# Mixer: VectorE runs the angle reduction behind the third chunk's states instead of ahead of them

## The chip, the cores and the metric

The kernel runs on one core of a Trainium2 chip. The metric is the device time of one execution in microseconds; the median of the runs is compared. The core has TensorE (PE, with its weight loads as PEld), VectorE (DVE), ScalarE (ACT), GpSimd (POOL) and SyncE (SP), whose queue issues every DMA here. Each engine works through its own instructions in order; semaphores tie them together.

## The reference

The input is x of shape (16, 512, 128). Six blocks are applied one after another: a feed-forward (FFN) block, attention, the same FFN, a mixture FFN, a state-space mixer, and the mixture FFN again. The part around the change is the mixer:

```python
proj = x @ W_in                                  # z, x_raw, B, C, dt_raw, lam_raw, theta
x_raw = silu(x_raw)
Bm, Cm = rms(B) * B_norm_bias, rms(C) * C_norm_bias
dt = clip(softplus(dt_raw + dt_bias), 0.0001, 0.5)
ang = -cumsum(mean(dt, -1) * theta, axis=1)      # 32 angles per token
cos, sin = cos(ang), sin(ang)
Cr, Br = rope(Cm, cos, sin), rope(Bm, cos, sin)
alpha = exp(dt * A); lam = sigmoid(lam_raw)
# chunked scan: S = decay * S + state of the chunk; y = intra + inter part
y = rms(y * silu(z)) @ W_out
```

and the mixture FFN, whose eight experts are relu(x @ W_e + b_e), summed with weights counted over the whole input.

## The kernel before, in words

Three phases follow each other: `attention_phase` (first FFN, attention, second FFN), `mixer_phase` (first mixture FFN and mixer), `last_ffn_phase`. The change touches only `mixer_phase`.

One batch is 512 tokens, four tiles of 128. The mixer phase runs 19 iterations, and each works on up to four batches at once: the experts of batch i (`ffn`), the preparation of batch i - 1 (`prep`: projection, step sizes, angles, rotation, scores), the scan of batch i - 2 (`scan`: four chunks), and the output of batch i - 3 (`tail`). From the third to the sixteenth iteration at least scan, preparation and experts are there together; in the seventeenth the experts are not.

The order of the work is written out by hand. `MIXER_AT` gives each step one or more slots from 0 to 82, and every engine walks through the slots of an iteration in turn (`for q in range(SLOTS)`) and issues what is due there. Within a slot VectorE takes tail, scan, ffn and prep in that order. The slots that matter here: `sums` 41, `angles` 49, `chunks` 50 (the third), `states` 56 (the third), `weights` 56, `own` 58 (the fourth), `experts` 59 and 64 (the last two), `products` 65 (the third), `rotate` 65, `chunks_rest` 66 (the third), `sumT` 68, `turn_y` 69, `own_p` 70, `diagonal_p` 71, `chunks` 73 (the fourth), `bt` 73.

- `sums` (TensorE, L1559): matmuls into banks 3 and 4 give the decay exponents, the summed angles (bank 4, columns 128 to 256) and the shifted weights.
- `angles` (VectorE, L1111): three clamps of the exponents to `mid`, then L1120 and L1121 read the angles from the bank to `ang` (the second with pi/2 added, for the cosine), then `reduce_angle` (L816): five operations in place on 128 x 256 elements, L819 to L823, each waiting for the one before it. The last signals `ang`.
- `decays` (ScalarE, L1347, slot 49): four Exp, then a table load (L1361), then the Sin (L1363), which waits for `ang`. Behind it in ScalarE's order stand `own_token` (L1366, slot 58) and the Relu of the last expert (L1396, slot 64).
- `states` (VectorE, L1171): for the two halves of a chunk a multiplication with the decay (L1179) and an addition of the chunk's matmuls from PSUM (L1186). `chunk_rest` on TensorE (L1615) waits for them, and `products` (L1191) on VectorE for `chunk_rest`.
- `add_experts` (GpSimd, L1484, slot 64) adds the last Relu to the one before; `sumT` on TensorE (L1704) sums the experts through matmuls with the identity (L1711) and waits for it.
- `rotate`: VectorE (L1135) and GpSimd (L1468) each multiply and add one half; VectorE then copies (L1145) when GpSimd's half is there, and TensorE transposes the result (L1579).
- `diagonal` on GpSimd (L1479) multiplies B and C (L1481).

On VectorE, `wait(ins)` counts the instruction on the semaphore `dve` and waits for it; `mark(ins)` only counts it and returns the count.

Of the kernel before, what the change touches and what calls it, by code (L numbers as in the profile page):

```python
# [18 lines left out]
ALU = mybir.AluOpType  # L19
# [796 lines left out]
def reduce_angle(v, wait, r, k):  # L816


    wait(v.tensor_scalar(k, r, float(1 / (2 * np.pi)), ROUND, ALU.mult, ALU.add))  # L819
    wait(v.tensor_scalar(k, k, ROUND, None, ALU.subtract))  # L820
    wait(v.scalar_tensor_tensor(r, k, -TWO_PI_HI, r, ALU.mult, ALU.add))
    wait(v.scalar_tensor_tensor(r, k, -TWO_PI_LO, r, ALU.mult, ALU.add))
    return v.tensor_scalar(r, r, PI_F32, -PI_F32, ALU.min, ALU.max)  # L823
# [93 lines left out]
def layer1_views(place):  # L917
# [17 lines left out]
    "gated": (34, 44, 73, 80), "squares": (25, 45, 66, 75), "mean": (35, 66, 77, 82), "mean_read": 82,  # L935
    "experts": (15, 17, 22, 25, 36, 44, 59, 64), "sumT": 68, "y": 71, "stats2": 73, "xn2": 74, "turn2": 80,
    "low2": 82, "project": (1, 2, 3, 6), "gates": 11, "shift": 7, "soft": 15, "steps": 34, "norm_bc": 15, "sums": 41,
    "angles": 49, "weights": 56, "rotate": 65, "diagonal": 74, "diagonal_p": 71, "bt": 73, "scores": 75, "mask": 78,
}


def mixer_phase(nc, x_in, n_in, x_out, n_out, w, ew, cnt_acc):
# [4 lines left out]
    with ExitStack() as ctx:  # L947
        def sb(name, shape, dt=F32):
            return ctx.enter_context(nc.sbuf_tensor("m_" + name, shape, dt))
# [25 lines left out]
        ang, angk, sc = (sb(n, [P, 2, NT, M_HEADS]) for n in ("ang", "angk", "sc"))  # L975
# [5 lines left out]
        bt = sb("bt", [P, 2, NT, 2, P])  # L981
# [27 lines left out]
        S = {n: ctx.enter_context(nc.semaphore("m_" + n)) for n in [*PER, "x_in0", "x_in1", "x_out0", "x_out1", "n_in0", "n_in1", "n_out", "dve", "pool", "start", "counted", "weights", "rate"]}  # L1009
# [3 lines left out]
        AT = MIXER_AT  # L1013
# [8 lines left out]
        def all_of(name, b):  # L1022
            return PER[name] * (b + 1)

        def batches(i):

            return [b if 0 <= b < BATCH else None for b in (i, i - 1, i - 2, i - 3)]

        with nc.Block(no_gpsimd_drain=True) as block:
# [25 lines left out]
            def _(dve):  # L1055
                v, done = nc.vector, [0]

                def mark(ins):
                    done[0] += 1
                    ins.then_inc(S["dve"], 1)  # L1060
                    return done[0]

                def wait(ins):
                    dve.wait_ge(S["dve"], mark(ins))
# [46 lines left out]
                def angles(b):  # L1111
                    dve.wait_ge(S["prep_ps"], all_of("prep_ps", b))
                    pa = ps[:, 4, 128:256].rearrange("p (t h) -> p t h", t=NT)
                    v.tensor_scalar(mid[:, 0], ps[:, 3, 384:512].rearrange("p (t h) -> p t h", t=NT),
                                    CLAMP, None, ALU.min)
                    v.tensor_scalar(mid[:, 2], ps[:, 3, 384:512].rearrange("p (t h) -> p t h", t=NT),
                                    -CLAMP, None, ALU.max)
                    v.tensor_scalar(mid[:, 1], ps[:, 4, 0:128].rearrange("p (t h) -> p t h", t=NT),
                                    CLAMP, None, ALU.min).then_inc(S["mid"], 1)
                    v.tensor_copy(ang[:, 0], pa)  # L1120
                    wait(v.tensor_scalar(ang[:, 1], pa, float(np.pi) / 2, None, ALU.add))  # L1121
                    reduce_angle(v, wait, ang[:, :], angk[:, :]).then_inc(S["ang"], 1)

                def source_weights(b):
# [83 lines left out]
                def mean_square(b):  # L1208
                    dve.wait_ge(S["ms_mm"], all_of("ms_mm", b))
                    v.tensor_scalar(ms[:, :], ps[:, 5, 256:264:2], 1.0 / D_INNER, RMS_EPS, ALU.mult,  # L1210
                                    ALU.add).then_inc(S["ms"], 1)

                def output(b):
                    dve.wait_ge(S["wo"], all_of("wo", b))
                    dve.wait_ge(S["rms"], all_of("rms", b))
                    if b >= 2:
                        dve.wait_ge(S[f"x_out{b % 2}"], 16 * (b // 2))
                    for t in range(NT):
                        ins = v.scalar_tensor_tensor(y2[:, b % 2, t, :], ps[:, 5, P * t:P * t + P], rms[:, t:t + 1],
                                                     y[:, b % 4, t, :], ALU.mult, ALU.add)  # L1220
                    ins.then_inc(S["y2"], 1)
# [23 lines left out]
                wait(v.tensor_scalar(w["w_in"][:], w["w_in"][:], W_SCALE, None, ALU.mult))  # L1245
                wait(v.tensor_copy(w["w_in_hl"][:, 0], w["w_in"][:]))
                v.tensor_tensor(w["w_in_hl"][:, 1], w["w_in"][:], w["w_in_hl"][:, 0], ALU.subtract).then_inc(S["weights"], 1)
                coef_done = [0, 0]
                for i in range(ITERATIONS):
                    ffn, prep, scan, tail = batches(i)  # L1250
                    for q in range(SLOTS):
                        if tail is not None:
                            if q == AT["out"]:
                                output(tail)
                            if q == AT["stats_gate"]:
                                dve.wait_ge(S["y2"], all_of("y2", tail))
                                statistics(y2[:, tail % 2], 1, S["var2"])
                            if q == AT["gate"]:
                                dve.wait_ge(S["gate"], all_of("gate", tail))
                                v.tensor_tensor(gl[:, :, :], ps[:, 5, 0:NT * EXPERTS].rearrange(  # L1260
                                    "p (t e) -> p t e", t=NT), w["gate_b"][:, :, :], ALU.add).then_inc(S["gate_read"], 1)
                            if q == AT["top"]:
                                dve.wait_ge(S["gate_read"], all_of("gate_read", tail))
                                top_two(v, dve, S["dve"], mark, gl, g8, gix, gif)
                                count_choices(v, dve, S["dve"], mark, gif, onehot, w, cnt_acc)
                        if scan is not None:
                            if q in AT["variants"]:
                                variants(scan, AT["variants"].index(q))
                            if q in AT["states"]:
                                states(scan, AT["states"].index(q))  # L1270
                            if q in AT["products"]:
                                products(scan, AT["products"].index(q))
                            if q in AT["gated"]:
                                gated(scan, AT["gated"].index(q))
                            if q == AT["mean_read"]:
                                mean_square(scan)
                        if ffn is not None:
                            if q in AT["experts"] and AT["experts"].index(q) % 2 == 0:
                                expert(ffn, AT["experts"].index(q))
                            if q == AT["low2"]:  # L1280
                                dve.wait_ge(S["xh"], all_of("xh", ffn))
                                v.tensor_tensor(xhl[:, 1], ps[:, 2, :], xhl[:, 0], ALU.subtract).then_inc(S["xl"], 1)
                            if q == AT["y"]:
                                dve.wait_ge(S["sumT"], all_of("sumT", ffn))
                                dve.wait_ge(S[f"x_in{ffn % 2}"], 16 * (ffn // 2 + 1))
                                v.scalar_tensor_tensor(y[:, ffn % 4], ps[:, 2, :].rearrange("p (t d) -> p t d", t=NT), 1.0 / EXPERT_SCALE,
                                                       x[:, ffn % 2], ALU.mult, ALU.add).then_inc(S["y"], 1)
                            if q == AT["stats2"]:
                                dve.wait_ge(S["y"], all_of("y", ffn))
                                statistics(y[:, ffn % 4], 0, S["var"])  # L1290
                        if prep is not None:
                            if q == AT["shift"]:
                                shift_dt(prep)
                            if q == AT["steps"]:
                                steps(prep)
                            if q == AT["angles"]:
                                angles(prep)
                            if q == AT["weights"]:
                                source_weights(prep)
                            if q == AT["rotate"]:  # L1300
                                rotate(prep)
                            if q == AT["diagonal"]:
                                diagonal(prep)
                            if q == AT["mask"]:
                                mask_scores(prep)
# [681 lines left out]
```

## Time and profile before

| | |
|---|---|
| median of 3 runs | 2549.31 us (2544.57 to 2550.05) |
| profiled execution | 2546.41 us, span 2544.6 us |
| mean granted TensorE clock | 0.946 of full speed |
| busy in the span | PE 85%, DVE 72%, POOL 57%, ACT 55%, PEld 40% |
| instructions | 39733 |
| attention phase | about 0 to 1625 us |
| mixer phase | about 1625 to 2437 us |
| last FFN phase | about 2437 to 2545 us |

The shares are averages over three phases. In the mixer the rows of one iteration show the order of the work. A row of the order of time has the start in us, the duration in us, engine, line, operation, what is written from what with the shapes, and how many instructions are merged; in brackets stands how long the engine was idle before it, and which instruction ended that.

### The profile page before, as it was taken

How to read it: one execution, taken by the hardware profiler on the slowest of the kernel's cores; microseconds unless marked ns; L12 is line 12 of the kernel's file. 1: busy time of each engine (PE TensorE's matmuls, PEld its weight loads, DVE VectorE, ACT ScalarE, POOL GpSimd, SP SyncE). 2: the span in 40 equal slices, each digit the busy share in tenths (PEclk: the TensorE clock that was granted, in tenths of full speed). 3: DMA queues.
4: the chain of work that ended last, by engine and by line, in shares of the span. 5: the costliest groups of instructions: out<-in, count | busy, mean ns of one | idle time of the engine just before them, and what ended most of it. 6: DMA issues, size and time to landing. Idle time of an engine off the chain costs nothing. (4 is left out here: it accounts for less than half of the span.)

```text
span 2544.6 us, 39733 instructions
## 1 busy us (share of the span) xinstructions
PE 2163.0 (85%) x14116; PEld 1006.0 (40%) x14116; DVE 1832.3 (72%) x4240; ACT 1410.1 (55%) x2651; POOL 1454.1 (57%) x1264
## 2 busy tenths in 40 slices
PE   3689989989989989988988988478888888888778
PEld 1223323323323323333323322246566565665544
DVE  5777777777777776776776772268888887887558
ACT  2166566566566566566566566254655545546235
POOL 3365665665665665665665645145655555555358
PEclk9799999999999999999999999589999999999779
DMA  3221212112112112112112110100000000000033
GB/s 115 54 49 41 48 34 51 43 34 55 38 34 63 30 34 63 30 34 63 36 35 52 42 56 9 33 11 24 26 22 26 22 26 22 23 17 18 10 99 108
DMA packets 86598, 103.70 MB, mean 41 GB/s; under 512 B 10240, under 2 KB 68736, under 8 KB 86272
## 3 DMA queue, kind: packets, MB, share of 16 engines
q1 hardware_dynamic: 86400, 101.16, 15.1%
q8 instruction: 113, 1.85, 0.3%
q14 instruction: 85, 0.70, 0.1%
HBM read 29.55 MB, written 20.97 MB: 20 GB/s over the span
## 5 line engine op out<-in xcount | busy, mean ns | idle before, releaser
L347 DVE TENSOR_REDUCE mS<-ps 128x1 f32<-128x512 f32 x1024 | 676.2, 680 | 303.2 <-PE ps L724 298.8
L506 ACT ACTIVATE pr<-ps 128x512 f32<-128x512 f32 x1024 | 585.7, 597 | 382.9 <-PE ps L708 365.5
L579 POOL TENSOR_TENSOR prs<-pr 128x512 f32<-128x512 f32 x384 | 487.4, 1288 | 243.7 <-ACT pr L506 243.7
L708 PE MATMUL ps<-qst,kst 97*128 97x512 f16 x1024 | 397.5, 391 | 53.2 <-ACT pr L506 52.1
L724 PE MATMUL ps<-kst,qst 96*128 96x512 f16 x1024 | 401.4, 393 | 36.6 <-DVE mS L347 25.5
L746 PE MATMUL ps<-pr,vt 128*32 128x512 f32 x2048 | 279.3, 618 | 0.0
L708 PEld LDWEIGHTS ps<-qst,kst 97*128 97x128 f16 x1024 | 99.0, 98 | 418.1 <-ACT pr L506 307.7
L583 POOL TENSOR_TENSOR terms<-terms 128x512 f32<-128x512 f32 x128 | 162.5, 1270 | 68.8 <-DVE terms L340 68.8
L340 DVE TENSOR_TENSOR terms<-ps,shared 128x512 f32<-128x512 f32 x256 | 172.8, 677 | 34.9 <-POOL lo L588 28.1
L588 POOL TENSOR_TENSOR lo<-terms,hi 128x512 f16<-128x512 f32 x128 | 148.0, 1157 | 76.9 <-ACT hi L486 76.9
L724 PEld LDWEIGHTS ps<-kst,qst 96*128 96x128 f16 x1024 | 101.2, 99 | 151.0 <-DVE mS L347 81.0
L486 ACT CAST hi<-terms 128x512 f16<-128x512 f32 x128 | 78.8, 616 | 113.3 <-POOL terms L583 113.3
L755 PE MATMUL ps<-prs,ones 128*32 128x512 f32 x768 | 107.3, 632 | 33.7 <-POOL prs L579 33.7
L1394 ACT ACTIVATE m_sqy<-m_yzT 128x256 f32<-128x256 f32 x64 | 26.5, 414 | 191.9 <-DVE m_yzT L1205 191.9
L665 PE MATMUL ps<-xnh,wq 128*128 128x512 f16 x256 | 99.6, 393 | 30.5 <-DVE terms L340 21.6
L1491 POOL TENSOR_TENSOR m_own<-m_own 128x256 f32<-128x256 f32 x64 | 78.5, 1227 | 78.6 <-ACT m_own L1372 78.6
L1164 DVE TENSOR_TENSOR m_xv<-m_xr,m_coef 128x1536 f32<-128x1536 f32 x64 | 118.5, 1854 | 0.0
L1533 PE MATMUL m_ps<-m_xe,ew_hl 128*128 128x512 f16 x384 | 106.1, 397 | 9.7 <-DVE ew_hl L1240 4.2
L1486 POOL TENSOR_TENSOR m_rl<-m_rl 128x512 f32<-128x512 f32 x32 | 60.3, 1886 | 92.9 <-ACT m_rl L1398 92.9
L563 POOL TENSOR_TENSOR rstd<-veps,minus_half 128x8 f32<-128x8 f32 (+1 forms) x38 | 55.1, 1450 | 96.5 <-DVE veps L313 96.5
L665 PE MATMUL ps<-xnh,wk 128*128 128x512 f16 x256 | 97.2, 382 | 12.4 <-DVE terms L340 12.4
L1625 PE MATMUL m_ps<-m_xv,m_gs 128*32 128x256 f32 x1024 | 74.3, 411 | 36.5 <-DVE m_state L1186 36.4
(265 smaller groups left out, 4381.8 us busy)
## 6 DMA issues: line engine op xcount, KB each, us to landing
qst<-hi SPq DMA_DIRECT2D x128, 128.0 KB, 2.3
kst<-hi SPq DMA_DIRECT2D x128, 128.0 KB, 2.4
qst<-lo SPq DMA_DIRECT2D x64, 128.0 KB, 2.3
kst<-lo SPq DMA_DIRECT2D x64, 128.0 KB, 2.4
x<-in_q SPq DMA_DIRECT2D x16, 256.0 KB, 2.8
shared<-in_rope SPq DMA_DIRECT2D x1, 4096.0 KB, 14.5
x<-yold SPq DMA_DIRECT2D x16, 256.0 KB, 2.5
n<-kept SPq DMA_DIRECT2D x16, 256.0 KB, 2.1
```

The lines of the kernel that those rows point to most:

```text
L340: v.tensor_tensor(terms[:, p % 2, c, :], ps[:, 4 + c, :], w["rope"][:, 2 * kq + c, g, :], ALU.mult).then_inc(S["pair_free"], 1)
L347: v.tensor_reduce(mS[:, b % 2, t, s:s + 1], ps[:, 2 + n % 2, :], AX, ALU.max).then_inc(S["s_read"], 1)
L506: a.activation(pr[:, s % 2, g, :], ps[:, g % 2, :], ACT.Exp, scale=ATT_SCALE).then_inc(S["exp"], 1)
L579: g.tensor_tensor(prs[:, c, :], pr[:, 0, c, :], pr[:, 1, c, :], ALU.add).then_inc(S["prs"], 1)
L583: g.tensor_tensor(terms[:, p % 2, 0, :], terms[:, p % 2, 0, :], terms[:, p % 2, 1, :], ALU.add).then_inc(S["rot"], 1)
L588: g.tensor_tensor(lo[:, p // NG, p % NG, :], terms[:, p % 2, 0, :], hi[:, p // NG, p % NG, :], ALU.subtract).then_inc(S["lo"], 1)
L665: ins = mm(out, lhs[a], rhs[b], start=k == 0, stop=k == 2)
L708: mm(ps[:, g % 2, :], kst[:, h, P * kt:P * kt + P], qst[:, h, :], start=True, stop=True).then_inc(S["st"], 1)
L724: mm(ps[:, 2 + n % 2, :], qst[0:3 * DH, h, P * t:P * t + P], kst[0:3 * DH, h, :], start=True, stop=True).then_inc(S["s"], 1)
L746: ins = mm(ps[DH * g:DH * g + DH, 6, :], vt[:, kt, DH * h:DH * h + DH], pr[:, s % 2, g, :], start=kt == 0, stop=kt == NT - 1, skip_group_c ...
L755: ins = mm(ps[DH * g:DH * g + DH, 7, :], w["ones"][:, 0:DH], prs[:, g, :], start=n % 2 == 0, stop=n % 2 == 1, skip_group_check=True)
L1164: v.tensor_tensor(xv[:, t % 2].rearrange("p c h r q -> p c h (r q)"), xr[:, b % 2, t].rearrange("p (o h) r q -> p o h (r q)", o=1).to_broa ...
```

## The change

`reduce_angle` is taken out of `angles` and put into a function of its own, `reduce_angles`, with a slot of its own, `"reduce": 56`. On VectorE slot 56 holds the third chunk's `states`, then the reduction, then the `weights`. The wait of the reduction for L1121, the last read of the bank, is now put at the start of `reduce_angles`. The other engines' programs are unchanged; ScalarE still has the Sin in slot 49.

```diff
-    "angles": 49, "weights": 56, "rotate": 65, ...
+    "angles": 49, "reduce": 56, "weights": 56, "rotate": 65, ...
...
                     v.tensor_copy(ang[:, 0], pa)
-                    wait(v.tensor_scalar(ang[:, 1], pa, float(np.pi) / 2, None, ALU.add))
+                    angles_read[0] = mark(v.tensor_scalar(ang[:, 1], pa, float(np.pi) / 2, None, ALU.add))
+
+                def reduce_angles():
+                    dve.wait_ge(S["dve"], angles_read[0])
                     reduce_angle(v, wait, ang[:, :], angk[:, :]).then_inc(S["ang"], 1)
...
-                coef_done = [0, 0]
+                coef_done, angles_read = [0, 0], [0]
...
                             if q == AT["angles"]:
                                 angles(prep)
+                            if q == AT["reduce"]:
+                                reduce_angles()
                             if q == AT["weights"]:
                                 source_weights(prep)
```

## Rows read from the trace of the kernel before

**Rows 1.** Busy table, four of thirteen iterations: stretch, us, busy by engine, PEclk, DMA.
```profile
1717.04:1764.68 47.64, 42.36 (x378) 29.88 (x378) 38.21 (x102) 25.24 (x51) 26.76 (x24) 0.93 0.08 23
...
1994.97:2041.76 46.79, 40.98 (x378) 28.81 (x378) 38.66 (x102) 25.25 (x51) 26.73 (x24) 0.96 0.08 23
2041.76:2087.24 45.48, 39.43 (x378) 27.18 (x378) 37.55 (x102) 25.26 (x51) 26.91 (x24) 1.00 0.08 25
...
2271.72:2318.43 46.71, 40.92 (x378) 28.74 (x378) 38.66 (x102) 25.24 (x52) 26.74 (x24) 0.96 0.04 12
```

**Rows 2.** The same table around the expert sum, in two iterations.
```profile
1998.07:2002.27 4.20, 4.11 (x22) 4.11 (x23) 3.20 (x4) 0.00 (x0) 4.04 (x5) 0.59 0.00 0
2044.86:2049.06 4.20, 4.12 (x36) 4.09 (x36) 3.21 (x4) 0.00 (x0) 4.04 (x5) 1.00 0.02 4
```

**Rows 3.** Order of time on VectorE, from 2038.7 us.
```profile
2038.73 0.27 DVE L1120 COPY m_ang<-m_ps 128x128 f32<-128x128 f32 x1
2038.93 0.27 DVE L1121 TENSOR_SCALAR m_ang<-m_ps 128x128 f32<-128x128 f32 x1
2039.24 0.29 DVE L819 TENSOR_SCALAR m_angk<-m_ang 128x256 f32<-128x256 f32 x1
...
2040.82 0.29 DVE L823 TENSOR_SCALAR m_ang<-m_ang 128x256 f32<-128x256 f32 x1
2041.03 0.28 DVE L1179 TENSOR_TENSOR m_kept<-m_state,m_wh 128x128 f32<-128x128 f32 x1
...
2042.19 0.28 DVE L1125 TENSOR_TENSOR m_wgt<-m_dec,m_ps 128x128 f32<-128x128 f32 x1
...
2042.99 0.74 DVE L1083 SCALAR_TENSOR_TENSOR m_acc<-m_ps,negb,m_acc 128x512 f32<-128x512 f32 x1
2043.85 0.69 DVE L1195 TENSOR_TENSOR m_pt<-m_ps,m_dec 128x512 f32<-128x512 f32 x1
2044.46 2.12 DVE L1139 TENSOR_TENSOR m_rp<-m_bcn,m_sc 128x384 f32<-128x384 f32 x2
```

**Rows 4.** Order of time on ScalarE, from 2040.4 us.
```profile
2040.47 1.28 ACT L1361 ACT_TABLE_LOAD   x1
2041.76 0.42 ACT L1363 ACTIVATE m_sc<-m_ang 128x256 f32<-128x256 f32 x1
...
2042.88 0.67 ACT L1398 ACTIVATE m_rl<-m_ps,posb 128x512 f32<-128x512 f32 x1
```

**Rows 5.** Order of time on GpSimd, the last experts' addition.
```profile
2043.62 1.26 POOL L1486 TENSOR_TENSOR m_rl<-m_rl 128x512 f32<-128x512 f32 x1 [4.61 <-ACT m_rl L1398]
```

**Rows 6.** Order of time on TensorE, from 2039.0 us.
```profile
2039.02 1.47 PE L1533 MATMUL m_ps<-m_xe,ew_hl 128*128 128x512 f16 x6
2042.33 1.07 PE L1625 MATMUL m_ps<-m_xv,m_gs 128*32 128x256 f32 x16 [1.84 <-DVE m_state L1186]
...
2044.94 0.49 PE L1711 MATMUL m_ps<-shared,m_acc 128*128 128x128 f32 x2 [0.62 <-POOL m_rl L1486]
```

**Rows 7.** Order of time on VectorE, the copy behind the rotation.
```profile
2048.81 0.73 DVE L1145 COPY m_br<-m_br 128x256 f32<-128x256 f32 x1 [0.95 <-POOL m_br L1477]
```

**Rows 8.** VectorE beside GpSimd in two iterations; durations (min/median/max) of L1139.
```profile
2050.07 0.28 DVE L1179 TENSOR_TENSOR m_kept<-m_state,m_wh 128x128 f32<-128x128 f32 x1
2050.06 1.42 POOL L1481 TENSOR_TENSOR m_gdp<-m_br 128x512 f32<-128x512 f32 x1
...
2280.05 1.37 DVE L1179 TENSOR_TENSOR m_kept<-m_state,m_wh 128x128 f32<-128x128 f32 x1
2280.01 1.26 POOL L1481 TENSOR_TENSOR m_gdp<-m_br 128x512 f32<-128x512 f32 x1
...
L1139 DVE TENSOR_TENSOR m_rp<-m_bcn,m_sc x32: 546/1092/1614, 1676.1 to 2368.4; 128x384 f32<-128x384 f32 x32
```

**Rows 9.** Order of time in the seventeenth iteration, TensorE and VectorE.
```profile
2364.49 1.94 PE L1625 MATMUL m_ps<-m_xv,m_gs 128*32 128x256 f32 x16 [4.27 <-DVE m_state L1186]
...
2367.13 0.69 DVE L1195 TENSOR_TENSOR m_pt<-m_ps,m_dec 128x512 f32<-128x512 f32 x1 [1.70 <-PE m_ps L1633]
```

More of the change, by code:

```diff
@@ L937 @@
     "low2": 82, "project": (1, 2, 3, 6), "gates": 11, "shift": 7, "soft": 15, "steps": 34, "norm_bc": 15, "sums": 41,
-    "angles": 49, "weights": 56, "rotate": 65, "diagonal": 74, "diagonal_p": 71, "bt": 73, "scores": 75, "mask": 78,
+    "angles": 49, "reduce": 56, "weights": 56, "rotate": 65, "diagonal": 74, "diagonal_p": 71, "bt": 73, "scores": 75, "mask": 78,
 }
```

## The prediction, made before the changed kernel ran

> **What bounds the kernel now.** I read the page's shares first, then the busy table by iteration of the mixer, then the order of time of each engine through one iteration, and last the waits inside it. The profiled execution took 2546.41 us around a span of 2544.6 us. The change touches only the mixer, which here runs from about 1625 to 2437 us; the attention stage before it and the last feed-forward stage behind it stay as they are. The reader is to see first that the mixer is a chain of iterations of almost constant length: from the Sin of the second iteration (1717.04) to that of the fifteenth (2318.43) there are thirteen, 601.4 us in all, 46.26 us each. They come in two kinds: six at 45.46 to 45.48 us with the TensorE clock at 1.00 (2.4 GHz), and seven at 46.71 to 47.64 us with a mean granted clock of 0.93 to 0.96 [rows 1]. In six of those seven the clock stands at 0.5 (1.2 GHz) around the matmuls of line 1711 that sum the experts: 0.59 over 4.2 us against 1.00 at the same place of a short iteration, and the same stretch holds 22 matmuls instead of 36 [rows 2]. The seventh has it elsewhere.
>
> No engine is full: TensorE is busy 39.4 of 45.48 us, VectorE 37.6 [rows 1]. So the time is in hand-overs, and I follow the one the change touches. I take the iteration whose Sin starts at 2041.76; the other steady ones repeat it within 0.02 us at these places.
>
> On VectorE the angles' last read of the bank starts at 2038.93, the five operations of the reduction start from 2039.24 and the last of them starts at 2040.82 and ends at 2041.11; then come the four operations of the third chunk's states (2041.03), the weights (2042.19), an expert (2042.99), the products (2043.85), the rotation (2044.46) [rows 3]. On ScalarE the table load ends at 2041.75 and the Sin starts at 2041.76: **today the Sin waits for its table, not for the angles**, which have been ready for 0.65 us. Behind the Sin, in ScalarE's queue, stand the own-token scaling and the Relu of the last expert, which starts at 2042.88, 1.12 us behind the Sin [rows 4]. TensorE finished that expert's product at 2040.49 [rows 6], so the Relu is late only because of its queue. GpSimd has waited 4.61 us for this Relu; it adds it (2043.62 to 2044.88) and only then goes on with its half of the rotation [rows 5]. TensorE waits 0.62 us for the same addition before its sum of the experts at 2044.94 [rows 6]. VectorE waits 0.95 us for GpSimd's half before it copies at 2048.81 [rows 7]. So all three meet again on one chain: Sin, own, Relu, addition, then the expert sum on TensorE and the rotation on GpSimd. The 1.84 us that TensorE waits for the states [rows 6] is a longer gap, but it ends on small matmuls (from 2042.33), behind which TensorE stands again until the addition lets it go on at 2044.94.
>
> **The change, part by part.**
> Nothing is added or removed: each iteration has the same nine operations, five of the reduction and four of the states, and the wait of L819 on the last read is now put ahead of the group.
>
> (a) The states move ahead of the reduction. The block from the first of them to the weights lasts 2042.19 - 2041.03 = 1.16 us, and the reduction 2041.03 - 2039.24 = 1.79 us [rows 3]. After the change the states start about 0.20 us behind the read at 2038.93 (independent operations of this size start 0.20 apart), at 2039.13, and are over by 2040.38 rather than 2042.28. The chunk's matmuls that they need are issued before the last six expert products, which start at 2039.02 [rows 6], so no wait takes the place. TensorE's part with the states then starts right behind the expert, near 2040.55, 1.8 us earlier than today. The 1.84 us are taken out there, but TensorE then stands until the addition. Gain on the path: nothing. The 0.11 us that VectorE saves, since the states run where the first step of the reduction had waited for its read, lets the weights start at 2042.08.
>
> (b) The reduction starts at 2040.29 and its last step at 2041.87, ending at 2042.16, that is 1.05 us later. Of these, 0.65 us go into the slack behind the table load. With a hand-over of 0.04 us the Sin starts at 2042.20: **0.44 us later**. Behind it are queued own, Relu, addition, rotation and expert sum, each by the same 0.44 us. Bounds: 0.40 us with no hand-over, 0.6 us if the 0.11 us aren't saved. Later in the iteration the four engines all continue from points shifted by it (VectorE from its copy, TensorE from the sum, GpSimd from the addition, ScalarE from the Relu), so I find no cover that absorbs it. Fourteen iterations have states and a sum of experts at once: 14 x 0.44 = +6.2 us.
>
> (c) Where the clock falls. Between the last expert product and the expert sum TensorE has only small matmuls, with waits of 1.84 and 0.62 us, 4.45 us in all (2040.49 to 2044.94). This is what the engine did before the clock is lowered in rows 2. The stretch becomes 4.45 + 0.44 = 4.89 us, with the waits joined into one near 2.8 us. A lowered iteration costs 46.79 - 45.48 = 1.31 us [rows 1]. Bounds: all seven unlowered ones also fall (7 + 1 of 14, 8 x 1.3 = +10 us), or none falls any more (six fewer, -8 us). A stretch that grows should be hit more often; I take two or three more, +3.2 us.
>
> (d) Exclusion between VectorE and GpSimd. The multiplication L1179 takes 0.28 us when it starts 0.01 us behind GpSimd's L1481, and 1.37 us when it starts 0.04 us behind: one runs, the other waits for its end [rows 8]. The change brings such a pair together: the addition now starts at 2042.20 + 1.86 = 2044.06; the products no longer wait for TensorE and start behind the expert, at 2042.88 + 0.74 - 0.08 = 2043.54 (0.08 us is by how much the products and the rotation overlap today), so the rotation L1139 starts 0.61 us behind them, at 2044.15. GpSimd is 0.09 us ahead, and by rows 8 0.04 us was enough for it. Then the rotation waits as it does today, at no cost. I take zero; the other end is a rival below. The Trainium skill, page "SBUF — State Buffer", section "SBUF: two separate sides", says that the pair of ports which the two engines share is an exclusive lock, held for a whole instruction by whoever starts first. Rows 8 agree, but for two starts within 0.01 us, where the later one was served; taken strictly, the rule gives the addition the port here too, and the sum stays.
>
> (e) The last iteration with a scan has no experts. There TensorE waits 4.27 us for the states and VectorE then 1.70 us for TensorE [rows 9], so here the earlier states are a gain: the products start about 1.9 us earlier, but the Sin and GpSimd's rotation are 0.9 us later, and VectorE's part must interleave with it. I take -1.0 us (between -1.7 and +0.9). The first iteration has no states: 0.
>
> **Sum:** +6.2 + 3.2 + 0 - 1.0 = +8.4 us on the 2546.41 us of the profiled execution, 2554.8 us. The median of the runs shown is 2549.31 us (2544.57 to 2550.05), 2.9 us above that execution, and +8.4 on it gives 2557.7 us. I forecast between the two: 2556 us.
>
> **The rivals.**
> 1. The delay alone: as forecast, but no more lowered iterations. +6.2 - 1.0 = +5.2 us, 2551.6 to 2554.5, about 2553 us. For it: the clock's pattern in rows 1 is alternating and may simply stay so. Against: the stretch before the sum grows.
> 2. The rotation wins the port. If L1139 reaches it before the addition, it runs its 0.55 us first (its shortest, [rows 8]), the addition ends 0.5 us later still, and with it the expert sum: 0.94 us per iteration. 14 x 0.94 = 13 us, nearly every iteration lowered (+8), -1: about +19, 2566 us. For it: the margin is 0.09 us, made of nine spacings. Against: rows 8 at 0.04 us.
> 3. The other side, a gain through the clock. With TensorE's matmuls of the chunk directly behind the expert products, the 1.84 us gap is gone from there; if that is the gap which brought the clock down, the six or seven lowered iterations end: -8 to -9 us against +5.2, near -3.5: 2543 to 2546 us, and against the median a gain of up to 6. It decides from four avoided falls on (5.2 / 1.31). Against: TensorE doesn't work more, the wait only moves behind the chunk.
> 4. No visible change: the 0.44 us disappear in a later wait of the iteration. 2546 to 2551 us. Against: a lowered iteration shows that what comes late at the sum of the experts is still there at its end (1.31 us, [rows 1, 2]).
>
> **How the numbers follow.** Forecast 0.50, rival 1 0.14, rival 2 0.18, rival 3 0.08, rival 4 0.10. What a measurement of this kernel can tell from no change is about 0.2%, 5.1 us, so slower means over 2554.4. Slower: 0.45 of the forecast, 0.18 of rival 2, 0.02 of rival 1: 0.65. Faster (under 2544.2): 0.05 of rival 3 and 0.01 of rival 4: 0.06. Within: 0.29. The range takes in rivals 1 and 2 and the upper part of rival 4: 2549 to 2567 us.
>
> **What would show it.** Right: the Sin starts 0.04 us behind the last step of the reduction, no longer behind the table load; TensorE's wait for the states (1.84 us) is gone and the one for GpSimd's addition grows from 0.62 to near 3 us; undisturbed iterations last 45.9 us instead of 45.48; nine or ten of thirteen have a lowered clock at the expert sum. Wrong: an unlowered iteration of 45.5 us or less (step b), fewer lowered iterations (step c), or an addition of 1.8 us on GpSimd instead of 1.26 (step d).

## The result, and the profile after

The changed kernel takes 2560.41 us (median of 6 runs, 2554.58 to 2561.16) against 2548.32 us before (6 runs, 2538.65 to 2552.9): a ratio of 1.005, 95% interval 1.0028 to 1.0072. It is slower by 12 us, inside the predicted range. The profiled execution took 2561.03 us, its span 2559.2 us (14.6 more than before). In the experiments, two executions stand far off (3138.36 us, the kernel before; 5177.73 us, the changed order with the Sin last and the fill); the ratios leave them out, and they move no median by more than 0.3 us.

The order of time on VectorE, in the iteration that answers to [rows 3]:

```profile
2045.88 0.28 DVE L1121 TENSOR_SCALAR m_ang<-m_ps 128x128 f32<-128x128 f32 x1
2046.08 0.28 DVE L1182 TENSOR_TENSOR m_kept<-m_state,m_wh 128x128 f32<-128x128 f32 x1
...
2047.24 0.29 DVE L819 TENSOR_SCALAR m_angk<-m_ang 128x256 f32<-128x256 f32 x1
...
2048.82 0.29 DVE L823 TENSOR_SCALAR m_ang<-m_ang 128x256 f32<-128x256 f32 x1
2049.03 0.28 DVE L1128 TENSOR_TENSOR m_wgt<-m_dec,m_ps 128x128 f32<-128x128 f32 x1
...
2051.08 2.88 DVE L1142 TENSOR_TENSOR m_rp<-m_bcn,m_sc 128x384 f32<-128x384 f32 x2
```

The states run 0.20 us behind the last read, and the reduction ends 3.23 us behind the start of that read, where it had been 2.18 us: 1.05 us later, as worked out. On ScalarE ([rows 4]), GpSimd ([rows 5]) and TensorE ([rows 6]):

```profile
2047.42 1.28 ACT L1366 ACT_TABLE_LOAD   x1
2049.14 0.42 ACT L1368 ACTIVATE m_sc<-m_ang 128x256 f32<-128x256 f32 x1 [0.44 <-DVE m_ang L823]
...
2050.26 0.67 ACT L1403 ACTIVATE m_rl<-m_ps,posb 128x512 f32<-128x512 f32 x1
```

```profile
2051.01 1.26 POOL L1491 TENSOR_TENSOR m_rl<-m_rl 128x512 f32<-128x512 f32 x1 [5.05 <-ACT m_rl L1403]
```

```profile
2045.97 1.47 PE L1538 MATMUL m_ps<-m_xe,ew_hl 128*128 128x512 f16 x6
2047.38 1.07 PE L1630 MATMUL m_ps<-m_xv,m_gs 128*32 128x256 f32 x16
...
2052.32 0.49 PE L1716 MATMUL m_ps<-shared,m_acc 128*128 128x128 f32 x2 [2.95 <-POOL m_rl L1491]
```

ScalarE now stands 0.44 us behind its table load for the last step of the reduction. The Relu still starts 1.12 us behind the Sin, the addition 1.87. TensorE's 1.84 us for the states is gone, and its 0.62 us for the addition has become 2.95. By the busy table ([rows 1]; the last row is the thirteen iterations from the second Sin to the fifteenth in one, with their mean clock), an iteration whose clock stays up lasts 45.91 us, 0.43 more than before, and only two of thirteen are of this kind:

```profile
1765.92:1811.83 45.91, 39.37 (x381) 27.17 (x380) 38.14 (x102) 25.25 (x51) 26.91 (x24) 1.00 0.08 26
2001.00:2049.14 48.14, 41.84 (x381) 29.73 (x380) 38.35 (x102) 25.25 (x51) 26.74 (x24) 0.93 0.08 23
2049.14:2095.06 45.92, 39.37 (x381) 27.18 (x380) 38.14 (x102) 25.26 (x52) 26.91 (x24) 1.00 0.08 24
2284.76:2331.99 47.23, 40.93 (x381) 28.80 (x380) 38.15 (x102) 25.25 (x51) 26.90 (x24) 0.96 0.04 12
...
1718.70:2331.99 613.29, 530.51 (x4917) 372.88 (x4916) 503.20 (x1314) 328.28 (x663) 348.48 (x312) 0.96 0.07 22
```

The other eleven last 47.20 to 48.14 us, all with the clock at 1.2 GHz during part of the expert sum or all of it (six before). Where the 14.6 us of the span are: 613.29 - 601.39 = 11.9 in these thirteen iterations, 1.7 ahead of them (0.9 of it before the mixer has begun, which the change doesn't reach), 1.0 behind them.

### The profile page after: what moved, and what is told of

It is laid out like the page before. It is cut to its first block and busy times, and to the rows that moved or that the text cites. A ratio compares the mean times of both kernels' runs of the same rounds, so it can differ in the third digit from the quotient of the medians.

```text
span 2559.2 us, 39733 instructions
## 1 busy us (share of the span) xinstructions
PE 2172.5 (85%) x14116; PEld 1018.8 (40%) x14116; DVE 1844.0 (72%) x4240; ACT 1410.6 (55%) x2651; POOL 1453.6 (57%) x1264
## 5 line engine op out<-in xcount | busy, mean ns | idle before, releaser
L571 POOL TENSOR_TENSOR xn<-sq 128x256 f32<-128x256 f32 x64 | 45.8, 735 | 101.1 <-ACT sq L478 101.1
```

## The experiments

Two causes had to be told apart: the Sin's delay through ScalarE's queue, and the clock. An iteration is called lowered where the clock stands at 1.2 GHz at the expert sum; the counts are of the thirteen iterations from the second Sin to the fifteenth, in one profiled execution each. Line numbers shift with the edits. The experiments ran on three chips, each beside the kernel before, and the text gives that kernel's median once for each. A ratio is always to the kernel before on the same chip; it is not always the quotient of the two medians. Medians from different chips compare only roughly (that kernel's own are 2543 to 2548 us).

**The order alone undone.**

```diff
-    "reduce": 56
+    "reduce": 49
```

> The changed kernel with the reduction's slot set back to 49: the function is split and the wait on the last read stands at its start, but the order on VectorE is that of the kernel before. Theory (all of the loss is the place behind the states): unlowered iterations 45.48 us, about six of thirteen lowered at the expert sum, a ratio to the kernel before of 1.000 within 0.003. Rival (the split itself costs): 45.6 us or more.

2543.33 us (11 runs) against 2543.01 (17 runs on the same chip), ratio 0.9997 (0.9986 to 1.0009). Unlowered iterations 45.48 us, thirteen iterations in 601.40 us against 601.39 before, six lowered, and these are the same six of the thirteen as in the kernel before. The split costs nothing; the whole loss is the place. The clock's part doesn't rest on one profile alone: the mean granted clock was 0.942 to 0.951 in these eleven executions and 0.937 to 0.943 in the six of the changed kernel.

**The clock held up by filling matmuls**, in the changed kernel and, with `FILL = {65: 6, 67: 2}`, in the one before.

```diff
+FILL = {67: 8}
...
+                            if q in FILL:
+                                if ffn:
+                                    pe.wait_ge(S["xl"], all_of("xl", ffn - 1))
+                                for _ in range(FILL[q]):
+                                    mm(ps[:, 2, :], w["w_in_hl"][:, 0, 0:P], w["w_in_hl"][:, 0, 0:512], start=True, stop=True)
                             if q == AT["sumT"]:
```

> The changed kernel with eight fp16 matmuls of 128 x 512 on constant operands added on TensorE in slot 67, between the mean square and the expert sum, written to the sum's own bank before it is started anew (no result changes). At 0.21 us each they fill 1.7 of the 2.95 us that TensorE waits there, so they delay nothing at 2.4 GHz. Theory (part of the loss is the lowered clock at the expert sum, brought on by the longer light stretch before it): no iteration is lowered there any more, all thirteen last 45.9 us as the two unlowered ones do, 13 x 45.91 = 597 instead of 613 us: total near 2544 to 2546 us. Rival (the clock follows from something else, or the sum isn't bound by it): about eleven of thirteen iterations stay at 47.2 us, total 2560 us.

> The kernel before with the same kind of matmuls: six in slot 65, in the 1.84 us wait for the states (1.3 us), and two in slot 67, in the 0.62 us wait for the addition (0.43 us). Theory: the six iterations lowered at the expert sum go, thirteen at 45.5 us are 591 to 592 instead of 601 us, total near 2539 us; and its distance to the filled changed kernel is the delay of the Sin alone, 14 x 0.43 less the gain of the last iteration: 5 to 6 us. Rival (the whole loss of 12 us is the delay in another form and not the clock): the distance of the two filled kernels stays 12 us.

2536.05 us (12 runs; ratio to before 0.9937, 0.9909 to 0.9966) and 2531.41 us (10 runs; 0.9913, 0.9878 to 0.9948), beside 2547.12 us of the kernel before (33 runs, of which 21 took 2538 to 2550 us and 12 took 2561 to 2570; none of the 22 runs with the fill is over 2542). TensorE's row of the fill in the first, and the busy table of an iteration and of the thirteen in each:

```profile
2038.46 0.61 PE L1661 MATMUL m_ps<-m_ones,m_sqy 128*128 128x2 f32 x4
2038.93 1.89 PE L1716 MATMUL m_ps<-w_in_hl 128*128 128x512 f16 x8
2042.02 0.49 PE L1724 MATMUL m_ps<-shared,m_acc 128*128 128x128 f32 x2 [1.20 <-POOL m_rl L1494]
```

```profile
2038.84:2084.74 45.90, 41.11 (x389) 27.81 (x389) 38.13 (x102) 25.26 (x51) 26.91 (x24) 1.00 0.08 26
...
1715.74:2315.79 600.05, 537.67 (x5021) 362.09 (x5021) 496.29 (x1314) 328.36 (x663) 349.81 (x312) 0.99 0.07 23
```

```profile
2032.81:2078.30 45.49, 41.17 (x387) 27.80 (x386) 37.57 (x102) 25.26 (x51) 26.93 (x24) 1.00 0.08 24
...
1714.03:2305.74 591.71, 535.29 (x5019) 361.50 (x5018) 488.36 (x1314) 328.47 (x664) 350.03 (x312) 1.00 0.08 23
```

No iteration is lowered at the sum in either. The changed kernel loses 24 us of its median by adding work, more than the 14 to 16 expected: part of that I can't place, as its thirteen iterations fell by 13.2 us only (two of them, of 47.4 us, have the low clock some 31 us behind the Sin, where the gate is computed), and the two medians come from different occasions. The delay stays: 45.90 against 45.49 us. The filled kernels are 4.6 us apart, with the 5 to 6 expected, where the unfilled ones are 12.1 (on another occasion). So somewhat over half of the loss is the clock; in the thirteen iterations of the unfilled profiles it is 6.3 of 11.9 us.

**The Sin out of the Relu's way** (`"sine": 64`, issued behind the Relu of that slot), in both orders.

```diff
-                    act.wait_ge(S["ang"], all_of("ang", b))
+
+                def sine(b):
+                    act.wait_ge(S["ang"], all_of("ang", b))
...
+                            if q == AT["sine"]:
+                                sine(prep)
```

> The changed kernel with one more edit: ScalarE issues the Sin in slot 64 behind the last expert's Relu, and not in slot 49 ahead of the own-token scaling and the Relu. Theory (the loss goes through ScalarE's queue: Sin, own, Relu, addition, expert sum): own starts at the end of the table load, the Relu 0.76 us earlier than in the changed kernel, the Sin some 1.0 us later but still ahead of GpSimd's rotation; unlowered iterations last 45.91 - 0.76 = 45.15 us, and the reduction's place costs nothing. Rival (the loss goes through the angles themselves: Sin, rotation, transposes): the Sin comes later still, iterations last 46.5 us or more, total above 2565 us.

> The kernel before with the same edit on ScalarE (Sin in slot 64). Theory: the Relu starts 0.33 us earlier than before, unlowered iterations last 45.48 - 0.33 = 45.15 us, the same as in the changed kernel with the Sin last; with the Sin out of the way the two orders on VectorE differ by less than 0.1 us per iteration. Rival (the earlier states are worth something by themselves): the changed kernel with the Sin last is shorter by up to the 1.84 us of TensorE's wait; or (the angles bind) this one gets slower, 46.4 us.

ScalarE's order in the first, and the busy tables of an unlowered iteration and of the thirteen in both:

```profile
1997.80 1.28 ACT L1366 ACT_TABLE_LOAD   x1
1999.09 0.91 ACT L1379 ACTIVATE m_own<-m_xr,m_gd 128x256 f32<-128x256 f32 x2
1999.91 0.67 ACT L1405 ACTIVATE m_rl<-m_ps,posb 128x512 f32<-128x512 f32 x1
2000.47 0.40 ACT L1370 ACTIVATE m_sc<-m_ang 128x256 f32<-128x256 f32 x1
```

```profile
2046.95:2092.11 45.16, 39.36 (x378) 27.18 (x378) 37.38 (x102) 25.26 (x52) 26.89 (x24) 1.00 0.08 25
...
1721.61:2329.62 608.01, 534.65 (x4914) 376.92 (x4914) 488.45 (x1315) 328.18 (x665) 348.62 (x312) 0.96 0.07 22
```

```profile
2078.11:2123.29 45.18, 39.43 (x386) 27.18 (x378) 37.25 (x102) 25.26 (x53) 26.93 (x24) 1.00 0.08 24
...
1711.00:2306.83 595.83, 521.80 (x4922) 360.22 (x4914) 489.29 (x1315) 328.42 (x665) 349.61 (x312) 0.98 0.07 23
```

The Sin starts 0.95 us later than in the changed kernel (1.39 us behind the end of the table load instead of 0.44) and the iteration gets shorter: 45.16 us, as worked out, where the rival wanted 46.5. The chain is the Relu's, not the angles'. And unlowered iterations are equal in both orders within 0.05 us, so the reduction's place costs nothing once nobody queues behind the Sin. The totals are less clear: 2552.83 us (12 runs, ratio 1.0005, 0.9975 to 1.0035) and 2538.94 us (12 runs; seven between 2533 and 2540 us, five between 2559 and 2568; ratio 0.999, 0.9949 to 1.0032). By their intervals neither differs from the kernel before, nor is one shown to differ from the other. The two profiles do: 608.0 against 595.8 us in thirteen iterations, with ten lowered against four. But the second profile is that of its quickest execution (2533.38 us), the first that of its second slowest (2557.68 us). Over all executions, the mean granted clock was 0.930 to 0.941 in all twelve of the first; in the second it was 0.945 to 0.949 in the seven short ones and 0.929 to 0.938 in the five long ones. So with the changed order the mean clock was low every time, with the order of before in five of twelve: a sign that the changed order draws the low clock even without the delay, and not more than a sign, since the kernel before spread in the same way on this chip.

**The same pair with the clock held**: the fill of slot 67 (eight) in the changed order, of slots 65 and 67 (six and one) in the order of before.

> The changed kernel with the Sin behind the Relu and eight filling matmuls ahead of the expert sum (they fit into the 2.2 us wait there). Theory: 45.16 us per iteration, none lowered at the sum, total near 2531.4 - 14 x 0.33 = 2527 us: so the 14 us between the two kernels with the Sin last were the clock alone. Rival (the early states cost something besides the clock): 2533 us or more.

> The order of the kernel before, with the Sin behind the Relu and filling matmuls (six ahead of the chunk's part with the states, one ahead of the expert sum). Theory: 45.2 us per iteration, none lowered at the sum, within 2 us of the changed kernel treated alike (2522.3 us): with the queue behind the Sin emptied and the clock held, the place of the reduction is worth nothing either way. Rival (the early states gain something once the Sin isn't in the way): 2525 us or more.

2522.27 us (6 runs, ratio 0.9915, 0.9896 to 0.9933; the kernel before 2545.2 us) and 2526.9 us (6 runs, ratio 0.9938, 0.9925 to 0.995; the kernel before 2543.01 us); 45.20 us per iteration in both, thirteen in 589.38 and 587.88 us, none lowered at the sum (one of the first at the gate). The first came 4.7 us below the 2527 us expected. The second missed its theory in the total: the medians differ by 4.6 us, where 2 were allowed, and 2526.9 lies in the region that the rival named. But the two ran on different chips, the intervals of the ratios overlap, and the iterations, in which the rival's gain would have to be, are equal. In the profiles, 1.8 us apart, the changed order is 2.2 us later at the fifteenth Sin and 4.1 us shorter behind it; why stays open. Both are below both kernels.

**A longer delay.**

```diff
-    "reduce": 56
+    "reduce": 57
```

> The changed kernel with the reduction one slot later, behind the weights too, so that the Sin is later by the two weight operations, 0.32 + 0.48 = 0.80 us. Theory (every 0.1 us of the Sin is 0.1 us of the iteration): unlowered iterations 45.91 + 0.80 = 46.7 us; and since the rotation (1.93 us behind the old Sin) now reaches the shared port about 0.7 us before the addition, the addition may lose it for up to 0.3 us: 46.7 to 47.0 us. Total near 2560 + 14 x 0.8 = 2571 us or somewhat more. Rival (0.44 us was a step, by the port or by a wait, and not a slope): 45.9 us and 2560 us.

2573.04 us (5 runs, ratio 1.011, 1.009 to 1.0129), 2571 us or somewhat more expected. ScalarE and GpSimd, then VectorE's rotation and the busy table:

```profile
1959.89 0.42 ACT L1368 ACTIVATE m_sc<-m_ang 128x256 f32<-128x256 f32 x1 [1.23 <-DVE m_ang L823]
```

```profile
1961.75 1.41 POOL L1491 TENSOR_TENSOR m_rl<-m_rl 128x512 f32<-128x512 f32 x1 [5.83 <-ACT m_rl L1403]
```

```profile
1961.03 1.02 DVE L1142 TENSOR_TENSOR m_rp<-m_bcn,m_sc 128x384 f32<-128x384 f32 x2
```

```profile
2056.05:2103.94 47.89, 40.64 (x378) 28.53 (x378) 37.54 (x102) 25.26 (x51) 26.50 (x24) 0.96 0.07 23
```

The Sin waits 1.23 us instead of 0.44, the 0.79 us that were put ahead of it. All thirteen iterations are lowered (47.9 to 49.8 us), so the slope can't be read from an unlowered one; 47.9 is 0.7 above the common lowered 47.2 us of the changed kernel. The thirteen last 628.87 us, 15.6 more than in the changed kernel; 13 x 0.79 = 10.3 of these are the Sin's. Here the rotation starts ahead of the addition: it takes 1.02 us for two operations instead of 2.88, and the addition 1.41 instead of 1.26.

**Where TensorE waits.** To see whether it is the length of the light stretch or its arrangement that brings the clock down, the chunk's matmuls were held back to where they had been, with the Sin still late.

```diff
+                            if q == AT["chunks_rest"][2] and prep is not None:
+                                pe.wait_ge(S["wgt"], all_of("wgt", prep))
                             if q in AT["chunks_rest"]:
```

> The changed kernel, and TensorE starts the third chunk's part with the states only when VectorE has written the weights (a wait on the semaphore wgt added). That puts these matmuls back to some 2.4 us behind the chunk's turn, as before the change, with a wait ahead of them and a short one (near 1.1 us) behind, while the Sin stays 0.44 us late. Unlowered iterations: 45.9 us in any case. Theory A (what lowers the clock more often is where the waits lie: joined to one right ahead of the expert sum): the count of iterations lowered at the sum goes back to about the six of thirteen of the kernel before, total near 2554 us. Theory B (it is the length of the light stretch, 4.45 to 4.89 us, as I predicted): the count stays at ten or eleven and the total at 2560 us.

```profile
1996.43 1.07 PE L1630 MATMUL m_ps<-m_xv,m_gs 128*32 128x256 f32 x16 [1.92 <-DVE m_wgt L1128]
...
1999.40 0.49 PE L1718 MATMUL m_ps<-shared,m_acc 128*128 128x128 f32 x2 [0.98 <-POOL m_rl L1491]
```

2558.2 us (6 runs, ratio 1.0058, 1.0039 to 1.0077), thirteen iterations in 614.1 us, nine lowered. The waits are back in two parts and the time isn't: arrangement alone (theory A, 2554 us and six lowered) falls. Length alone doesn't seem to do either, by the pair above. In six profiles, with the stretch between the expert products and the expert sum ("early" means right behind the expert products):

```
stretch, us     chunk's matmuls late     early
4.15            4 of 13 lowered          10 of 13
4.45            6                        -
4.88            9                        11
5.82            -                        13
```

The rows are the two kernels with the Sin last, the kernel before, this version with the changed kernel, and the later reduction. In each column a longer stretch has more lowered iterations, and in each row with both the early matmuls have more. That is one execution each, and the 4 of the first row is of the quickest of a wide spread. That both count is the reading that fits best; it is not shown. What decides it in a single iteration stays open.

**A version that gathers it**: own-token scaling moved to slot 38, the Sin last, fills of slot 67 (five) in the changed order, of 65 and 67 (six and one) in the order of before.

```diff
-    "own": (1, 2, 26, 58)
+    "own": (1, 2, 26, 38)
```

> The version that the experiments point to: reduction behind the states as in the changed kernel, the Sin behind the last Relu, the fourth chunk's own-token scaling moved from slot 58 to slot 38 on ScalarE (it fits into the 4.9 us wait there), five filling matmuls. The Relu then starts right behind the table load, 1.1 us ahead of the kernel before, the addition near 1.1 us earlier, and the expert sum and GpSimd's rotation with it: 44.4 to 44.7 us per iteration, none lowered at the sum, total 2515 to 2521 us. If another wait takes the place (the products and VectorE's rotation, which can't start before their turn), 45.0 us and 2526 us.

> The same with the own-token scaling in slot 38, the counterpart of the version that gave 44.69 us per iteration. Here TensorE's part with the third chunk's states ends at 2043.8 in the times of the kernel before, which is later than the addition (2043.75), and its fills and mean square push the expert sum to 2044.5: the early states should be worth something at last. Theory: 44.9 to 45.1 us per iteration against 44.69, total 3 to 5 us above the counterpart (2527.6), 2531 us. Rival: the same 44.7 us.

2527.63 us (6 runs, ratio 0.993, 0.9911 to 0.9949) and 2521.87 us (5 runs, ratio 0.9911, 0.9898 to 0.9924). The unlowered iteration is 44.69 and 44.82 us, so the early states are at last worth 0.13 us, where 0.2 to 0.4 were expected. Yet the totals go the other way: the first missed its 2515 to 2521 us by 6.6, and the second its 2531 us by 9, on the good side. They ran on different chips and the intervals overlap, so no order between them is shown. Three of the first's thirteen iterations (46.2 us) have the low clock at the gate, none of the second's. In the first the addition takes 1.55 us instead of 1.26, which costs 0.29 of the 1.1 us that it was to be earlier. The best kernels of the study, 2521.87 and 2522.27 us, are not told apart.

## Why the prediction was right

Forecast 2556 us, range 2549 to 2567, slower at 0.65; measured 2560.41. The sum said +8.4 us; the medians moved by 12.1 and the profiled spans by 14.6. The path was right and the number came near partly because the forecast was set between two starting points, 2554.8 and 2557.7; two terms of the sum were off, (c) in size and (e) in sign. In the order of the sum, +6.2 + 3.2 + 0 - 1.0 became, for the thirteen iterations, +5.6 + 6.3 + 0, and outside them +1.7 ahead and +1.0 behind.

- **(a), no gain from the early states:** right. The 1.84 us went, and the next wait took 2.33 us more, from 0.62 to 2.95.
- **(b), 0.44 us per iteration from the Sin:** right, 0.43. The Sin's hand-over was 0.03 us rather than 0.04. That it runs through the Relu was argued from the rows before; the two kernels with the Sin last show it.
- **(c), the clock:** the sign and the mechanism were right, the size too small. I took two or three more lowered iterations, +3.2 us; there were five more, and two of the lowered ones lasted 48.0 and 48.1 us. 13 x 0.43 = 5.6 of the 11.9 us are the delay and 6.3 the clock. My reason, that the stretch grows from 4.45 to 4.89 us, is probably only half of it: that the small matmuls now lie early seems to count too (ten against four at equal length, in one execution each).
- **(d), no cost at the port:** right, by a margin of 0.07 us (addition 2051.01, rotation 2051.08; I had 0.09). The addition kept 1.26 us. The later reduction shows the order of rival 2, but at 0.15 us and not 0.5: the rotation started 0.72 us ahead there and was through 0.30 us behind the addition's start. Rival 2's own sum was off as well: 13 + 8 - 1 is 20 us and not 19.
- **(e), -1.0 us in the last iteration with a scan:** not confirmed. What lies behind the fifteenth Sin grew by 1.0 us, with the clock low in other places before and after; TensorE's wait for the states there went from 4.27 to 2.36 us, the 1.9 us that were worked out, but not to the end of the kernel. I can't separate the two. In the two kernels with the fill alone, what lies behind that Sin is 1.27 us shorter in the changed order (223.82 against 225.09 us), the way that was forecast; but with the Sin last it is 1.5 us longer, with the fill too 4.1 us shorter, and with the own-token scaling moved 0.2 us longer, in one execution each. The sign of this term stays open.
- **Rival 3, a gain through the clock,** was the wrong way round: with the gap gone from behind the expert products the clock fell more often.
- **A name:** the prediction's "Sin of the second iteration" is the second Sin. It belongs to the third iteration of the mixer, since the first one prepares nothing.

## What to carry to other kernels

A wait of 1.84 us on the busiest engine was worth nothing here, because a later wait of the same engine ends on another chain; look at what releases the next one. Before an operation is moved behind another, look at who queues behind its consumer: here 0.65 us of slack behind a table load was all there was, and a Relu that had nothing to do with the angles paid for the rest. Where TensorE has idle stretches with only small matmuls, a few fp16 matmuls into a bank that is about to be started anew can be worth more than the reordering: here they took 24 us off the changed kernel, which had lost 12. And where a loss is partly the clock, look at several executions: one profile counts one of them.

## What the hardware showed unexpectedly

Eight matmuls without a use (1.89 us) took the changed kernel from 2560.41 to 2536.05 us, by runs on two occasions; against the kernel before on its own chips, from 1.005 to 0.9937. Between VectorE and GpSimd hundredths of a microsecond decide: L1179 at 0.01 us behind GpSimd's start ran at once, at 0.04 it lost 1.1 us ([rows 8]). All thirteen traces agree. Where the multiplication of the states started within 0.013 us of GpSimd's multiplication of B and C (127 pairs), it took 0.27 to 0.28 us and GpSimd's 1.40 to 1.43 us instead of 1.26; where it started 0.03 to 0.26 us behind (23 pairs), it took 1.16 to 1.38 us. No pair lies between the two.
